# Attention over a graph in split fp16: high weights against high and low values as one 512-column matmul, with a second add per tile

## What is computed

```python
h = relu(layernorm(x))                      # x: 4096 x 256, float32
q, k, v = h @ Wq.T + bq, h @ Wk.T + bk, h @ Wv.T + bv
a = q @ k.T / 16 + adj + adj                # adj: 4096 x 4096, float32, 64 MiB
y = x + softmax(a, axis=-1) @ v
```

## Time and profile before

| | us |
|---|---|
| median of 3 runs | 723.69 |
| lowest and highest of them | 722.16, 724.4 |
| the profiled execution, its time | 720.62 |
| the profiled execution, its span | 718.9 |

### The profile page before, as it was taken

One profiled execution on the slowest core, in us unless ns is written; L12 is line 12 of the kernel. 1 busy time (PEld: TensorE's weight loads), 2 busy tenths in 40 slices (PEclk: granted clock), 3 DMA queues, 4 the chain that ended last, 5 costly groups with the idle time before them and its releaser, 6 DMA issues.

```text
span 718.9 us, 14692 instructions
## 1 busy us (share of the span) xinstructions
PE 690.8 (96%) x4799; PEld 473.4 (66%) x4799; DVE 603.4 (84%) x1282; ACT 436.4 (61%) x732; POOL 432.9 (60%) x436
## 2 busy tenths in 40 slices
PE   4788999999999999999999999999999999999988
PEld 3555555567666667667667666666666666667766
DVE  4889777988897978788888888797988888888896
ACT  4799564665656555656656565656566666656530
POOL 1889603475655667474747556565738475655667
PEclk8799999999999999999999999999999999999999
DMA  8398588998879889898988897888879798878472
GB/s 284 119 279 234 142 223 224 258 252 229 251 207 258 223 230 232 237 240 226 269 208 246 235 254 217 241 216 243 239 217 266 205 256 231 250 217 225 121 187 75
DMA packets 93244, 161.06 MB, mean 224 GB/s; under 512 B 20976, under 2 KB 41840, under 8 KB 93168
## 3 DMA queue, kind: packets, MB, share of 16 engines
q1 hardware_dynamic: 68432, 126.41, 63.9%
q10 hardware_dynamic: 24736, 33.72, 18.3%
HBM read 80.35 MB, written 8.39 MB: 123 GB/s over the span
## 4 chain that ended last, share of the span: by engine, by line
PE 74%; DVE 10%; issue 4%; POOL 3%; DMA 2%; ACT 2%; ACTq 2%; SPq 1%; DVEq 0%; POOLq 0%
PE bank L1443 41%; PE bank L1504 33%; ACTq L789 2%; DVE rows L1128 2%; DVE rows L1101 1%; DMA xT<-rows 1%; DVE top L1137 1%; SPq L420 1%; DVE h_tile L1142 1%; POOL wT L625 1%; DVE stats L1046 1%; DVE rows L1094 1%; DMA rows<-in_x 1%; DMA g_pair<-g_scratch 1%; ACT rows L709 1%
## 5 line engine op out<-in xcount | busy, mean ns | idle before, releaser
L625 POOL TENSOR_TENSOR wT<-xT,wT 128x512 f16<-128x512 f32 x233 | 268.3, 1162 | 209.8 <-ACT wT L807 206.8
L1443 PE MATMUL bank<-v_sb,wT 128*128 128x256 f16 x2796 | 343.0, 273 | 0.2
L1504 PE MATMUL bank<-top,a_op 128*128 128x512 f16 x1344 | 330.8, 379 | 5.5 <-DVE chunk_max L1101 2.3
L1443 PEld LDWEIGHTS bank<-v_sb,wT 128*128 128x128 f16 x2796 | 273.3, 98 | 81.4 <-DVE xy L1191 1.3
L807 ACT CAST wT<-xT 128x512 f16<-128x512 f32 x233 | 139.6, 611 | 124.8 <-PE bank L1443 66.1
L1504 PEld LDWEIGHTS bank<-top,a_op 128*128 128x128 f16 x1344 | 130.6, 98 | 116.0 <-DVE chunk_max L1101 3.6
L778 ACT ACTIVATE rows<-rows,exp_bias,exp_scale 128x1024 f32<-128x1024 f32 x128 | 158.7, 1240 | 65.0 <-issue 31.0
L1101 DVE CUSTOM_DVE_ANT_0 rows<-bank,rows 128x512 f32<-128x512 f32 x256 | 173.6, 680 | 10.7 <-PE bank L1504 2.3
L1128 DVE STREAM_TRANSPOSE rows<-rows 128x1024 f32<-128x1024 f32 x128 | 158.3, 1239 | 5.8 <-ACT rows L778 5.5
L1086 DVE SCALAR_TENSOR_TENSOR rows<-rows,adj_scale,bank 128x512 f32<-128x512 f32 x64 | 47.7, 745 | 41.7 <-PE bank L1504 41.7
L769 ACT ACTIVATE rows<-rows,adj_scale 128x512 f32<-128x512 f32 x64 | 46.2, 722 | 36.0 <-POOL wT L625 20.7
(11 more groups left out here) (115 smaller groups left out, 478.8 us busy)
## 6 DMA issues: line engine op xcount, KB each, us to landing
rows<-in_adj SPq DMA_DIRECT2D x128, 512.0 KB, 5.9
xT<-rows SPq DMA_DIRECT2D x488, 64.0 KB, 3.2
xT<-rows ACTq DMA_DIRECT2D x488, 64.0 KB, 3.7
rows<-in_x SPq DMA_DIRECT2D x8, 512.0 KB, 5.5
xy<-in_x SPq DMA_DIRECT2D x32, 128.0 KB, 5.8
g_scratch<-xT SPq DMA_DIRECT2D x16, 256.0 KB, 3.4
g_pair<-g_scratch SPq DMA_DIRECT2D x15, 256.0 KB, 4.4
out_y<-xy SPq DMA_DIRECT2D x30, 128.0 KB, 5.7
```

Of the source, the lines that this page charges most:

```text
L625: nc.gpsimd.tensor_tensor(split_piece(m, 1), exchanged(m), split_piece(m, 0), ALU.subtract).then_inc(split_lo, 1)
L1443: return nc.tensor.matmul(out_ap, stationary, moving, start=first, stop=last)
L1504: last = nc.tensor.matmul(ps[:], s, mv, start=first and k == 0, stop=k == 2, skip_group_check=True)
```

## The change

It has four parts.

1. For 31 of the 32 tiles (`WIDE_TILES`), the two matmuls of a key block with the high weights become one over high and low values together, 512 columns into the whole bank. Its second half then holds high weights by low values. `add_low` adds that half to `y` with a further DVE instruction of 128 x 256 ahead of `finish`, and `finish` waits for it.
2. On DVE, `finish` of a tile goes from the end of its period (n modulo 4 = 2 or 3) to behind the first transpose of that period, with `add_low` ahead of that transpose. The `sums` of the odd tile go from the end of the period with n modulo 4 = 2 to the end of the one before.
3. On SP, the load of the queries goes ahead of the exchange and of the first refill.
4. In DVE's list for the last units, casts stand between transposes.

```diff
--- before.py
+++ after.py
@@ -46,6 +46,7 @@
 SETUP = 7
 LATE = 4 * (PERIODS - WEIGH_LAG) + 5
 LAST_UNITS = 3
+WIDE_TILES = TILES - 1
 B11, B21, B22, T3, T1, T2, T4 = range(7)
 A11, A12, A21, A22, S1, S2, S3, S4 = range(8)
 
@@ -237,6 +238,7 @@
         split_lo = sem("split_lo")
         weighed = sem("weighed")
         sum_step = sem("sum_step")
+        low_added = sem("low_added")
         y_done = sem("y_done")
 
         def wait(eng, s, value):
@@ -503,12 +505,12 @@
                     store(2 * (p - 3) + 1)
                 if n % QUADS in (0, 1) and 2 <= p < PAIRS:
                     load_xy(2 * p + n % QUADS)
+                if n % QUADS == 0 and p + 1 < PAIRS:
+                    load_g(p + 1)
                 if unit_in_range(u):
                     exchange_a(u)
                 if unit_in_range(u - 1):
                     refill(u - 1, 0)
-                if n % QUADS == 0 and p + 1 < PAIRS:
-                    load_g(p + 1)
                 if unit_in_range(u - 1):
                     refill(u - 1, 1)
                 if n % QUADS == 3 and p >= 2:
@@ -1182,8 +1184,21 @@
                 nc.vector.tensor_tensor(out_scale[:, one], inv_sum[:, one], inv_omega[:], ALU.mult
                                         ).then_inc(sum_step, 1)
 
+            def add_low(tile):
+                if tile >= WIDE_TILES:
+                    return
+                t = tile % 2
+                y = xy[:, tile % XY, :]
+                dve.wait_ge(sum_step, 3 * tile + 3)
+                dve.wait_ge(weighed, 4 * (tile_units(tile) + 1))
+                dve.wait_ge(xb_done, tile + 1)
+                nc.vector.scalar_tensor_tensor(y, o_ps[t][:, D:2 * D], out_scale[:, t:t + 1], y,
+                                               ALU.mult, ALU.add).then_inc(low_added, 1)
+
             def finish(tile):
                 t = tile % 2
+                if tile < WIDE_TILES:
+                    dve.wait_ge(low_added, tile + 1)
                 y = xy[:, tile % XY, :]
                 dve.wait_ge(sum_step, 3 * tile + 3)
                 dve.wait_ge(weighed, 4 * (tile_units(tile) + 1))
@@ -1382,7 +1397,12 @@
                     finish_11(n)
                 if n % QUADS == 0 and 1 <= p <= PAIRS:
                     bias(2 * p - 1)
+                done = 2 * p - 6 + n % QUADS
+                if n % QUADS >= 2 and p >= 2:
+                    add_low(done)
                 turn(u, 0)
+                if n % QUADS >= 2 and p >= 2:
+                    finish(done)
                 if scoring:
                     scores_22(n)
                     finish_22(n)
@@ -1393,11 +1413,8 @@
                     row_bias(2 * p + n % QUADS - 2)
                 if n % QUADS == 0 and p >= 2:
                     sums(2 * p - 4)
-                if n % QUADS == 2 and p >= 2:
-                    finish(2 * p - 4)
+                if n % QUADS == 1 and p >= 2:
                     sums(2 * p - 3)
-                if n % QUADS == 3 and p >= 2:
-                    finish(2 * p - 3)
 
             for n in range(SETUP, PERIODS):
                 period(n)
@@ -1410,30 +1427,37 @@
             turn(u, 0)
             turn(u, 1)
             late_high(LATE + 2)
-            sums(TILES - 4)
+            late_high(LATE + 3)
             turn(u + 1, 0)
             turn(u + 1, 1)
-            late_high(LATE + 3)
-            finish(TILES - 4)
+            sums(TILES - 4)
             late_high(LATE + 4)
             late_high(LATE + 5)
+            add_low(TILES - 4)
             late_high(LATE + 6)
             sums(TILES - 3)
+            finish(TILES - 4)
+            late_high(LATE + 7)
             turn(u + 2, 0)
+            late_high(LATE + 8)
             turn(u + 2, 1)
-            for m in range(LATE + 7, LATE + 11):
-                late_high(m)
+            late_high(LATE + 9)
             turn(u + 3, 0)
+            late_high(LATE + 10)
             turn(u + 3, 1)
+            late_high(LATE + 11)
+            add_low(TILES - 3)
+            late_high(LATE + 12)
             finish(TILES - 3)
-            for m in range(LATE + 11, LATE + 15):
-                late_high(m)
+            late_high(LATE + 13)
+            late_high(LATE + 14)
             sums(TILES - 2)
             for m in range(LATE + 15, LATE + 19):
                 late_high(m)
             sums(TILES - 1)
             for m in range(LATE + 19, 4 * PERIODS):
                 late_high(m)
+            add_low(TILES - 2)
             finish(TILES - 2)
             finish(TILES - 1)
 
@@ -1559,8 +1583,12 @@
                     block = 4 * part + k
                     kt = half * BLOCKS + block
                     w_hi = piece(m)[:, k, 0]
-                    matmul(o_ps[t][:, 0:D], w_hi, v_sb[:, kt, 0], half == 0 and block == 0, False)
-                    matmul(o_ps[t][:, 0:D], w_hi, v_sb[:, kt, 1], False, False)
+                    first = half == 0 and block == 0
+                    if 2 * p + t < WIDE_TILES:
+                        matmul(o_ps[t][:], w_hi, v_sb[:, kt].rearrange("p s d -> p (s d)"), first, False)
+                    else:
+                        matmul(o_ps[t][:, 0:D], w_hi, v_sb[:, kt, 0], first, False)
+                        matmul(o_ps[t][:, 0:D], w_hi, v_sb[:, kt, 1], False, False)
                 pe.wait_ge(split_lo, m + 1)
                 for k in range(KT):
                     block = 4 * part + k
```

## The result

| | before | after |
|---|---|---|
| median of 8 runs, us | 723.55 | 720.22 |
| lowest and highest, us | 722.16, 724.4 | 718.06, 722.67 |
| profiled execution, its time | 720.62 | 720.27 |
| profiled execution, its span | 718.9 | 718.5 |

The ratio is 0.9963, with a 95% interval of 0.9948 to 0.9978: faster, by 0.37%. Forecast were 718.3 us and 0.75%. In a later session the same kernel gave 718.12 against 722.89, ratio 0.9936 (0.992 to 0.9953). The sign and the range (714.5 to 722.2) held. In the first session the medians differ by 3.3 us of the 5.4 forecast (by the ratio it is half of the forecast: 0.37% of 0.75%); in the later one they differ by 4.8 us.

A forecast was written before the change was run, and what follows sets the result against it. TensorE, busy 96% of the span, was taken as the bound. Gains 2.4 + 1.3 + 0.3 - 0.1 + 1.5 = 5.4 us took 720.62 to 715.2; plus 3.07 to the median, 718.3 us, range 714.5 to 722.2.

The forecast's parts named there:

- the row load of quarter 2: SyncE's queue: row load lands 0.8 us later, so the tightest group loses; 0.1 us lost, bounds 0 to 1.
- the end: Last units: new order of casts and transposes on DVE shortens PE's work behind the last product; 1.5 us gained, bounds 0 to 3.4.
- The wide matmul: PE's weighing: four pairs of 256 columns become four matmuls of 512 at 215.7 ns each; 2.4 us gained.
- the fifth rival: PE: a wide matmul streams its second half for next to nothing; some 640 us with DVE binding; chance 0.01.
- add_low and finish ahead of line 1094: DVE, quarters 2 and 3: 0.80 us more ahead of line 1094 still ends 0.33 us before product 4; cost nothing.
- Finish and sums away from the end of quarter 2: DVE: moving them removes PE's stalls at the next period's first read; 1.3 us gained, bounds 0 to 2.6.
- The queries' load: SyncE's queue: load ahead of the exchange ends GpSimd's wait ahead of one late group; 0.3 us gained.
- The third rival: SyncE's queue: quarter 2's row load comes too late in every group; 7.7 us worse, 726.0 us; chance 0.06.
- the sign of being wrong that I had named: Last term counts as wrong if PE still loses over 3 us behind the last product.
- The carry from profile to median: Median of the three runs lay 3.07 us above the profiled execution; carried over, 715.2 becomes 718.3 us.
- the first (the end gives nothing, 719.8): Last units: casts and subtractions hand the port over as before, three extra vector instructions eat the rest; chance 0.14.

The follow-up runs named there:

- f2: Kernel before with only the queries' load moved ahead of the exchange; 722.76 us, ratio 1.0001 to before.
- e1: Wide matmul and add_low alone, every order as in the kernel before; 726.17 us against 722.97 before, ratio 1.005.
- e2: Full change with the queries' load put back at its old place behind the first refill; 723.05 us, ratio 1.0003 to before.
- e0: Kernel before, unchanged, run again for a second profile; 722.43 us.
- f1: Full change, unchanged, run again in a later session; 718.12 us, ratio 0.9936 to before.
- e3: Full change with finish of tile 29 directly behind its add_low, ahead of the next cast; 719.26 us, ratio 0.9941 to before.
- g1: Full change without wide matmul and add_low, all moves kept; 718.54 us against 722.45 before, ratio 0.9942.
- f3: Full change with the even tile's store moved to the head of quarter 3's SyncE list; 718.36 us, ratio 0.9934 to before.
- f4: Full change with the edits of f3 and e3, and the queries' load ahead of the load of x; 717.61 us, ratio 0.9925 to before.
- g2: Full change with the edits of f3 and e3, plus tile 28's sums and the fifth cast between unit 61's transposes; 715.80 us against 722.45 before, ratio 0.9898.

## Why the prediction was right or wrong

The time lay in the range, and the sign was right. By the profiles' stages two terms are missing of the gain: the row load of quarter 2 took some 1.6 us more than I gave it, and the end gave 1.4 us less.

*The wide matmul: right.* 9.77 - 9.73 = 0.04 us a period, as forecast, in every profile with it; 2.2 us over the 55 periods. This form of matmul keeps the product's pitch of 215.7 ns. That also settles the fifth rival: the 131 ns that the Trainium skill gives ("TensorE: Matmul & The Clock Gate", section Back-to-back issue gap) are not seen here in either stream.

*add_low and finish ahead of line 1094: right.* Product 4 never waited in quarters 2 and 3. In those periods it starts 0.41 to 0.42 us behind the end of line 1096's instruction (line 1094 of before), where I had 0.33 and before had 0.94.

*Finish and sums away from the end of quarter 2: right in kind.* No stall at a first read of quarter 3 in any kernel with the moves. I gave 1.3 us, and that is what the two profiles of before show in quarters 3 (f2 shows 3.1). But measured against the wide matmul without the moves it is 5.6 us, since add_low makes that pile 0.4 us longer. I never priced this alternative: without the moves the wide matmul makes the kernel slower (e1).

*The queries' load: wrong in reason.* I gave 0.3 us for one late group. The move is worth nothing in the kernel before by the medians and, inside the change, 1.6 to 3.0 us by the stages (539.54 against 537.95 and 536.54) and some 3 by the ratios (1.0003 against 0.9963), where GpSimd's wait would have grown from 30 to 45 us. I asked what the wait cost before, not what it would cost in the kernel that the other edits make. It grows by 15 us, or 1.1 us per pair: the load is issued 0.4 us later in the period, and its median time to landing is 5.2 us in e2 and 4.4 in before. In e1, with add_low and the old orders, the landing takes 5.1 us too, and the wait is 36.1 us. Why the landing takes longer stays open.

*The row load of quarter 2: right, and under-priced.* I named it, with 0.1 us lost and 0 to 1 as bounds. The waits rose from 0.8 us in the earlier trace rows (and 2.8 in e0) to 7.4, 9.3 and 11.1 us in three profiles with the change (after, f1, e3), and PE lost 0.9, 2.5 and 3.1 us in quarters 2. The bound should have been 3. e2 shows that the load's 0.4 us in the queue aren't what does it, and g1, with every move but no add_low, has waits of 3.4 us only. I counted 0.8 us of later issue and took the 4.9 us to landing as fixed. Quarter 0's first row load is issued, in the median over twelve pairs, 6.8 and 7.1 us behind that quarter's product 4 in before and e0, 7.5 in f2 and g1, and 7.6, 8.3 and 7.8 in after, f1 and e3. And it takes longer to land: 4.9 to 5.3 us in the eight profiles with the wide matmul, against 4.2 to 4.5 in before, e0, f2 and g1. That part I had left out. The third rival had this mechanism, at 7.7 us, with every group late. Why the landing is longer was not tested. f3 takes the lateness away by taking out the wait for the store's landing, which stood in the queue in before as well (64.4 us in 13 times; 64.5 in after).

*The end: the step that failed.* I summed DVE's list up to the cast at 698.72 and let PE follow GpSimd. The list itself came out: counted from the last product, that cast starts at 23.37 us in before and at 21.92 in after, 1.45 us earlier where I had 1.2. But PE didn't follow. "Nobody but the store and the next weighing of that bank waits for finish, and both get it earlier" is true in the steady part and false here: tile 31's first weighing is that next weighing, at the very place where I counted the gain, and in the new list finish of tile 29 stands behind add_low and a cast of 1.20 us. So 1.5 us were given and 0.1 came: PE still loses some 3.5 us there, which is the sign of being wrong that I had named. With finish ahead of that cast the end part is 0.7 us shorter in e3 and 1.1 in f4. The order itself is worth 2.1 us in g1, more than I gave it; add_low and the place of finish take some 1.2 of them back, and the later exponential 0.9.

*The carry from profile to median: right, without grounds.* I took 3.07 us over, which takes the gain off the median. The second profile of before was 1.8 us longer, for a lead-in 2.0 us longer, which the moves hardly touch; when I took the 3.07 over I didn't know where they lay.

Of the rivals, the first (the end gives nothing, 719.8) was nearest to the 720.22 of the first session, for another cause than it names. Summed by stages, before against after: steady 539.05 to 537.25 (mean of two each), end 40.25 to 40.13, so 1.9 us by profiles, 3.3 by the first set of medians and 4.8 by the second. Where the rest lies is not shown. The lead-in alone is an unlikely place: in every kernel with all the moves (e2 aside) the medians gain 0.6 us or more beyond the stages, and 27 runs of the kernel before spread over 7.1 us, more than the lead-in's 4.3. That other executions of before lose more in quarters 3 than its two profiles do, as f2's does, would fit and wasn't tested.

That g1 and the full change come out alike is shown by ratios of different sessions (0.9942 against 0.9936 and 0.9963) and by the stages (538.35 + 38.16 = 576.5 against 576.7 and 578.0). So on top of the moves the wide matmul gained nothing that can be measured here: its 2.2 us of pitch went back into the row waits and the end. In g2, where the row waits are gone, the steady part is 535.38 us, 2.1 less than 55 periods of 9.77 could be; there the wide matmul pays in that part. A g2 without it was not run, so what it is worth there in all stays open.

## What to carry to other kernels

Price each part of a change against the kernel that the other parts make, not against the kernel before: a wait of 30 us in all was nearly free in the one kernel, and one of 45 us cost 4 us in the other, and one added instruction of 0.4 us made the kernel 3 us slower without the moves that came with it. Where a list is rewritten, look for every wait on each moved instruction at that place, too, and not only in the steady part. And when profiles differ by less than the lead-in varies, compare them by stages between two instructions that both have.

## What was not expected of the hardware

The lead-in of one and the same kernel took 132.2 us in one execution and 135.9 in another, with no difference in work; some 1 us of it is the wait for the first load of x (6.0 against 7.1 us), the rest was not followed. Which cast DVE starts ahead of GpSimd's subtraction matters by a factor of three: two casts back to back took 0.77 us, one behind an instruction of 0.4 us took 1.20, as the subtraction had begun in between. And with the wide matmul and add_low the same loads took longer to land: quarter 0's row load 4.9 to 5.3 us where it was 4.2 to 4.5, the queries' load at its old place 5.1 and 5.2 us where it was 4.4. The cause is not known.
